# Query, key and relative rows of two attention layers: placed by DMA instead of by picks and moves

## The reference, cut to what matters

```python
q, k, v = heads(x @ wq + bq), heads(x @ wk + bk), heads(x @ wv + bv)     # 12 x 256 x 16 each
attn = einsum("bqd,bkd->bqk", q * scale, k)                               # 12 x 256 x 256
rel_h = einsum("bhwc,hkc->bhwk", q.reshape(12, 16, 16, 16), Rh)           # Rh[h, k] = rel_pos_h[h - k + 15]
rel_w = einsum("bhwc,wkc->bhwk", q.reshape(12, 16, 16, 16), Rw)
attn = attn.reshape(12, 16, 16, 16, 16) + rel_h[..., :, None] + rel_w[..., None, :]
out = softmax(attn.reshape(12, 256, 256)) @ v                             # back to 256 x 192, then @ wo + bo
...
x = x + L0(_gn(x)); x = x + L1(_gn(x))                                    # _gn: group norm, 32 groups
```

## Time and profile before

| | |
|---|---|
| median of 3 runs | 72.73 us (72.13 to 75.06) |
| the profiled execution's own time | 72.31 us |
| its span, first to last instruction | 70.6 us |
| mean granted TensorE clock | 0.992 |
| PE / ACT / DVE / GpSimd busy | 62.8 / 49.2 / 48.5 / 26.6 us |
| DMA | 1.75 MB in 1575 packets |

### The profile page before, as it was taken

One profiled execution on the slowest core, in us unless ns is written; L12 is line 12 of the kernel. 1 busy time (PEld: TensorE's weight loads), 2 busy tenths in 40 slices (PEclk: granted clock), 3 DMA queues, 4 the chain that ended last, 5 costly groups with the idle time before them and its releaser, 6 DMA issues.

```text
span 70.6 us, 1570 instructions
## 1 busy us (share of the span) xinstructions
PE 62.8 (89%) x574; PEld 51.5 (73%) x574; DVE 48.5 (69%) x110; ACT 49.2 (70%) x92; POOL 26.6 (38%) x61
## 2 busy tenths in 40 slices
PE   4996989999998999899997899999988998989950
PEld 4995869999767776655786769999766896555640
DVE  3789498999999993414258578999999886224420
ACT  2973194789999999992421096679999999993410
POOL 4846899998033135999405000000023132000000
PEclk9999999999999999999999999999999999999996
DMA  0789600000000000000000000000000000000003
GB/s 0 178 248 238 164 0 9 0 0 0 5 0 0 0 0 9 5 0 0 0 0 0 14 0 0 0 0 0 0 0 0 9 0 0 0 0 0 0 0 111
DMA packets 1575, 1.75 MB, mean 25 GB/s; under 512 B 344, under 2 KB 1178, under 8 KB 1568
## 3 DMA queue, kind: packets, MB, share of 16 engines
q1 hardware_dynamic: 1280, 1.49, 8.1%
q10 hardware_dynamic: 288, 0.16, 0.8%
HBM read 1.46 MB, written 0.20 MB: 23 GB/s over the span
## 4 chain that ended last, share of the span: by engine, by line
PE 56%; ACT 24%; DVE 12%; issue 4%
ACT pt L383 12%; PE ps L813 11%; ACT qs L336 10%; PE ps L681 5%; PE ps L728 5%; PE ps L596 4%; PE ps L794 4%; DVE zq L564 4%; PE ps L650 3%; PE ps L667 3%; PE ps L784 3%; PE ps L766 3%; PE ps L636 3%; PE ps L769 2%; PE ps L745 2%
## 5 line engine op out<-in xcount | busy, mean ns | idle before, releaser
L336 ACT ACTIVATE qs<-ps 64x512 fp32r<-64x512 f32 (+1 forms) x30 | 17.7, 590 | 0.8
L481 DVE TENSOR_REDUCE nm<-ps 128x2 f32<-128x512 f32 x24 | 15.5, 687 | 1.2 <-PE ps L681 0.8
L316 POOL CAST nmhl<-nm 128x4 fp32r<-128x4 f32 x12 | 2.3, 189 | 25.3 <-DVE nm L481 25.3
L681 PE MATMUL ps<-ks,qs 128*128 128x256 f32 x48 | 10.4, 305 | 0.9 <-DVE nm L481 0.3
L383 ACT ACTIVATE pt<-ps 128x1024 f32<-128x1024 f32 x10 | 10.3, 1027 | 0.2
L709 PE MATMUL ps<-qs,ks 128*128 128x256 f32 x48 | 9.4, 298 | 0.9 <-ACT qs L336 0.9
L681 PEld LDWEIGHTS ps<-ks,qs 128*128 128x128 f32 x48 | 7.1, 188 | 2.9 <-issue 2.6
L709 PEld LDWEIGHTS ps<-qs,ks 128*128 128x128 f32 x48 | 6.8, 189 | 1.7 <-issue 1.6
L794 PE MATMUL ps<-xn,win 97*128 97x256 f32 (+1 forms) x24 | 5.7, 385 | 1.3 <-DVE xn L542 1.3
L336 ACT ACTIVATE zq<-ps 64x256 fp32r<-64x256 f32 x6 | 2.3, 380 | 5.8 <-PE ps L794 5.7
L336 ACT ACTIVATE rr_hi<-ps 64x384 fp32r<-64x384 f32 x8 | 3.9, 485 | 3.3 <-PE ps L813 3.1
(11 more groups left out here) (105 smaller groups left out, 124.1 us busy)
## 6 DMA issues: line engine op xcount, KB each, us to landing
win<-in_w_in_dram SPq DMA_DIRECT2D x4, 216.0 KB
xt<-in_x_dram SPq DMA_DIRECT2D x2, 96.0 KB, 2.3
wout<-in_w_out_dram SPq DMA_DIRECT2D x2, 96.0 KB
wout<-in_w_out_dram SPq DMA_DIRECT2D x2, 48.0 KB
out_dram<-res ACTq DMA_DIRECT2D x1, 96.0 KB, 1.7
out_dram<-res SPq DMA_DIRECT2D x1, 96.0 KB, 1.7
rel_raw<-in_rel_dram ACTq DMA_DIRECT2D x1, 62.0 KB, 2.5
win<-in_w_in_dram SPq DMA_DIRECT2D x2, 2.2 KB
```

Source lines behind the costliest of these rows:

```text
L336: return act.activation(dst, src, ACT.Copy, scale=scale)
L481: dve.tensor_reduce(nm[:, p, a, :], ps[:, S_BANK[a], :].rearrange("p (t k) -> p t k", k=T), AX.X, ALU.max, negate=True).then_inc(max_sb, 1)
L681: last = mm(ps[:, S_BANK[a], t * T:(t + 1) * T], qs[:, 2 * p + a, t * P:(t + 1) * P], ks[:, 2 * p + a, :], start=True, stop=True)
```

## The change

- Picks and moves stay for the queries and keys of group 0 and for the relative terms of groups 0 and 1. The relative terms of group 0 now go to two banks and are moved in quarters (`("r", 0, odd, u)`, 64x256).
- The queries and keys of groups 1 and 2 are written by SP to DRAM tensors (`q_rows`, `k_rows`), twice each, since `qs` and `ks` hold every part twice, and read back into rows 0 to 63 of `qs` and `ks`.
- The relative terms of group 2 go from `rr_hi` and `rr_lo` straight to `qs`, by eight DMAs of 31 rows of 1 KB (SBUF to SBUF). GpSimd clears rows 64 and 65 of that group first (`clear_max_rows`).
- The output channels of the query and key weights are put in another order on the host (`by_channel`), so that a head's rows lie 4 apart.
- `values` goes from DVE to ACT; the maximum rows of pairs 3 and 5 go from ACT to DVE; a bias row of `ont` is set by GpSimd; the two normalising steps are split (`sums`, `normalise`).
- SP waits for the weights of layer 0 before it issues the loads behind them.
- The lists of PE, ACT and DVE get new orders.

```diff
+        K_BANK, Q_BANK, R0_BANK, R1_BANK = 1, 0, [2, 0], 1
-        ACT_MOVES = [("k", 0, 0), ("k", 1, 0), ("q", 1, 0), ("q", 1, 1), ("r", 0, 0), ("r", 1, 1),
-                     ("q", 2, 1), ("r", 1, 0), ("q", 2, 0), ("r", 2, 0), ("r", 2, 1), ("k", 2, 1)]
-        DVE_MOVES = [("q", 0, 0), ("q", 0, 1), ("k", 0, 1), ("k", 1, 1), ("r", 0, 1), ("k", 2, 0)]
+        ACT_MOVES = [("q", 0, 1), ("k", 0, 1), ("r", 0, 0, 0), ("r", 0, 1, 1), ("r", 1, 1), ("r", 1, 0)]
+        DVE_MOVES = [("q", 0, 0), ("k", 0, 0), ("r", 0, 1, 0), ("r", 0, 0, 1)]
+        MAX_ON_ACT, MAX_ON_DVE = [0, 1, 2, 4], [3, 5]
...
+        q_rows, k_rows = ([nc.dram_tensor(f"{name}_rows{l}", (64, G4, NG - 1, T), F32).ap() for l in range(LAYERS)]
+                          for name in "qk")
...
                 if l == 0:
+                    sp.wait_ge(ld_win[0], 48)
                     sp.dma_start(lora_ab[:, :, :], lora).then_inc(ld_lora, 16)
...
+            def queries_out(l):
+                sp.wait_ge(z_lo, 6 * l + NG)
+                for copy in range(2):
+                    sp.dma_start(q_rows[l][32 * copy:32 * copy + 32, :, :, :].rearrange("c j g t -> (c j) g t"),
+                                 zq[:, 1:NG, :].bitcast(F32)).then_inc(q_out, 16)
+
+            def keys_out(l, part):
+                sp.wait_ge((z_hi, z_lo)[part], 6 * l + 2 * NG)
+                for copy in range(2):
+                    first = 32 * part + 16 * copy
+                    sp.dma_start(k_rows[l][first:first + 16, :, :, :].rearrange("c j g t -> (c j) g t"),
+                                 zk[64 * part:64 * part + 64, 1:NG, :].bitcast(F32)).then_inc(k_out, 16)
+
+            def queries_in(l, g):
+                sp.wait_ge(q_out, 32 * (l + 1))
+                sp.dma_start(qs[0:64, G4 * g:G4 * g + G4, :].bitcast(F32),
+                             q_rows[l][:, :, g - 1, :]).then_inc(q_in[g - 1], 16)
+
+            def keys_in(l, g):
+                sp.wait_ge(k_out, 64 * (l + 1))
+                sp.dma_start(ks[0:64, G4 * g:G4 * g + G4, :].bitcast(F32),
+                             k_rows[l][:, :, g - 1, :]).then_inc(k_in[g - 1], 16)
+
+            def relative_in(l, part):
+                sp.wait_ge((rr_hi_sb, rr_lo_sb)[part], 4 * l + 4)
+                rr, first = ((rr_hi, 66), (rr_lo, 97))[part]
+                for j in range(G4):
+                    sp.dma_start(qs[first:first + R, 2 * G4 + j, :].bitcast(F32),
+                                 rr[G4 + j:P:G4, 2, :].bitcast(F32)).then_inc(r_in, 16)
+
+            for l in range(LAYERS):
+                queries_out(l)
+                keys_out(l, 0)
+                keys_out(l, 1)
+                for g in range(1, NG):
+                    queries_in(l, g)
+                    keys_in(l, g)
+                relative_in(l, 0)
+                relative_in(l, 1)
...
+            def clear_max_rows(l):
+                pool.wait_ge(rstd_sb, NC * (l + 1))
+                pool.memset(qs[64:66, 2 * G4:NH, :].bitcast(F32), 0.0).then_inc(max_zero, 1)
+                pool.wait_ge(max_zero, l + 1)
...
             def scores(l, p, a):
...
-                moved(l, *both("k", p // 2), *both("q", p // 2), *both("r", p // 2))
+                    moved(l, *both("k", 0), *both("q", 0))
+                if p < 2:
+                    moved(l, ("r", 0, 0, p), ("r", 0, 1, p))
+                elif p < 4:
+                    pe.wait_ge(q_in[0], 16 * (l + 1))
+                    pe.wait_ge(k_in[0], 16 * (l + 1))
+                    moved(l, *both("r", 1))
+                else:
+                    pe.wait_ge(q_in[1], 16 * (l + 1))
+                    pe.wait_ge(k_in[1], 16 * (l + 1))
+                    pe.wait_ge(r_in, 16 * 2 * G4 * (l + 1))
+                    pe.wait_ge(max_zero, l + 1)
```

More of the change, by code:

```diff
@@ L130, in attention_layers @@
         rstd_sb = sem("rstd_sb")
+        made_bias_row = sem("made_bias_row")
+        q_out, k_out, r_in, max_zero, nmt_dve, r0_ps = (sem(n) for n in (
+            "q_out", "k_out", "r_in", "max_zero", "nmt_dve", "r0_ps"))
+        q_in = [sem(f"q_in{g}") for g in range(1, NG)]
+        k_in = [sem(f"k_in{g}") for g in range(1, NG)]
         lora_zero, lora_sb = sem("lora_zero"), sem("lora_sb")
@@ L406, in _ @@
                 relative_rounded(l, 0)
+                move(l, 0)
                 relative_rounded(l, 1)
-                move(l, 0)
+                move(l, 1)
                 relative_rounded(l, 2)
-                move(l, 1)
                 relative_rounded(l, 3)
-                for n in range(2, 11):
-                    move(l, n)
+                move(l, 2)
+                move(l, 3)
+                move(l, 4)
+                values(l)
+                move(l, 5)
                 max_rows(l, 0)
-                move(l, 11)
                 max_rows(l, 1)
[L417 to L429, removed]
+                probabilities(l, 0)
+                max_rows(l, 2)
+                probabilities(l, 1)
+                probabilities(l, 2)
+                max_rows(l, 4)
+                probabilities(l, 3)
+                probabilities(l, 4)
+                last_probabilities(l, 0)
+                last_probabilities(l, 1)
+                last_columns(l)
+                turned(l, 0)
+                turned(l, 1)
             act.wait_ge(y_ps, NC + 1)
@@ L476, in normalise, with maximum, max_rows @@
                     rinv[:, g, :, :].unsqueeze(3).to_broadcast([P, TT, G4, D]), ALU.mult).then_inc(on_sb, 1)
[L478 to L482, removed]
+            def maximum(l, p, a):
+                dve.wait_ge(s_ps, NH * l + 2 * p + a + 1)
+                dve.tensor_reduce(nm[:, p, a, :], ps[:, S_BANK[a], :].rearrange("p (t k) -> p t k", k=T),
+                                  AX.X, ALU.max, negate=True).then_inc(max_sb, 1)
+            def max_rows(l, p):
+                dve.wait_ge(nmt_ps, PAIRS * l + p + 1)
+                dve.tensor_copy(*max_args(p)).then_inc(nmt_dve, 1)
             def relative_rest(l, n):
@@ L569, in _ @@
                 relative_rest(l, 1)
-                move(l, 2)
                 relative_rest(l, 2)
                 relative_rest(l, 3)
+                move(l, 2)
                 move(l, 3)
[L574 to L580, removed]
+                maximum(l, 0, 0)
+                maximum(l, 0, 1)
+                maximum(l, 1, 0)
+                maximum(l, 1, 1)
+                maximum(l, 2, 0)
+                maximum(l, 2, 1)
+                maximum(l, 3, 0)
+                maximum(l, 3, 1)
+                maximum(l, 4, 0)
+                maximum(l, 4, 1)
+                max_rows(l, 3)
+                maximum(l, 5, 0)
+                maximum(l, 5, 1)
                 out_columns(l, 0)
+                max_rows(l, 5)
+                out_columns(l, 1)
+                sums(l, 0)
+                sums(l, 1)
                 normalise(l, 0)
-                out_columns(l, 1)
                 normalise(l, 1)
+                sums(l, 2)
                 normalise(l, 2)
@@ L664, in relative_rows, with first_relative_rows @@
                 pick, rr, split = ((pick_rh, rr_hi, rr_hi_sb), (pick_rl, rr_lo, rr_lo_sb))[part]
                 pe.wait_ge(split, 4 * l + 4)
+                return mm(where, pick[:, 2 * u:2 * u + 2, :].rearrange("p j n -> p (j n)"), rr[:, g, :],
+                          stop=(part == 1), skip_group_check=True, **flags)
+            def first_relative_rows(l, part, u):
+                if part == 0 and u == 0:
+                    pe.wait_ge(pick_zero, 3)
+                    pe.wait_ge(z_lo, 6 * l + 6)
+                elif part == 0:
+                    moved(l, *both("q", 0))
+                last = relative_product(l, 0, part, u, ps[:, R0_BANK[u], 0:T], start=(part == 0))
+                if part == 1:
+                    last.then_inc(r0_ps, 1)
@@ L666, in relative_rows @@
+            def relative_rows(l, part):
+                if part == 0:
+                    moved(l, *both("k", 0))
                 for u in range(2):
-                    last = mm(ps[:, R_BANK[g], u * T:(u + 1) * T],
-                              pick[:, 2 * u:2 * u + 2, :].rearrange("p j n -> p (j n)"), rr[:, g, :],
-                              start=(part == 0 and u == 0), stop=(part == 1), skip_group_check=True)
+                    last = relative_product(l, 1, part, u, ps[:, R1_BANK, u * T:(u + 1) * T],
+                                            start=(part == 0 and u == 0))
```

171 lines of the change are left out of this document (84 added, 87 removed).

## The result

The kernel with the change takes 95.8 us, median of 4 runs (95.0 to 96.08), against 73.85 of the kernel before beside it (72.13 to 75.06). The ratio is 1.318, interval 1.313 to 1.324: slower by 32%. (The ratio leaves out the two slow executions of the kernel before, 74.97 and 75.06, since a program here has a second, slower state in some of its executions.) The profiled execution took 96.08 us, its span is 94.4; the span before was 70.6. So where 16 us more were forecast, 23 to 24 came. The sign, the place and the range held, the size did not.

What follows compares the result with a forecast made beforehand. Bound by when the first maximum starts, ACT's work and pair 4's first product, which eight one-engine DMAs would delay by 7.5 us: 72.3 + 2 x 7.5 + 2 x 0.5 = 88.3 us. Range 73 to 97, the forecast's own 79.7 to 96.7.

Steps and rivals of the forecast that it cites:

- Each of these DMAs runs on one engine, and all eight on the same: Group 2's relative rows: 31 is a prime, so 248 packets of 49 ns on one engine take 12.2 us.
- the spread: Rival for the eight 31-row DMAs: spread over 16 engines, two rows each, landing at 21.2; 66.9 us in all; chance 0.18.
- the serial case: Rival: the one-engine DMAs don't overlap and each pays 1.4 us of its own, 11 more per layer, 110 us; chance 0.02.
- The cheap packets: Rival: one engine, but SBUF to SBUF costs half, some 25 ns a packet, full at 24.4, 73.3 us; chance 0.06.
- The bounds of 38 and 60 ns: Price of a 1 KB packet on one engine, around the 49 taken: 248 packets from 9.4 to 14.9 us.
- They start behind group 2's reads, at 18.9: Start of the 31-row DMAs' data in SP's list, or an us earlier if writes run faster; `r_in` full at 31.4.
- the 12.2 of the sum: Time of the eight 31-row DMAs: 248 packets of 49 ns on one engine, 12.2 us.
- The 14.9: DRAM round trip: writes of queries and keys, issued from 10.3, data from 11.3, landed at about 14.9.
- between nothing and 2 us per layer: Behind the stall, products start at the 0.50 clock (1.2 GHz) after PE idles ten us; 0.5 us per layer taken.
- Hidden, by 1.3 us: Pair 2: group 1's reads landed at 17.7, wanted at 19.0, so the DRAM round trip costs nothing.
- so it costs nothing: SP's new wait for layer 0's weights puts the loads' issues off by some 3 us, to about 10.2, without cost.
- The first part: Less work on PE, ACT and DVE: 2.7 us gained per layer if every DMA came in time, lost in the stall.

Runs made afterwards that it cites:

- E2: Changed kernel with four DMAs of 64 or 60 source rows, onto 16 or 15 rows of four heads, for the eight of 31: 75.09 us, ratio 1.037.
- E3: Changed kernel with the first four 31-row DMAs left whole and the last four each cut into 16 and 15 rows: 87.53 us.
- E1: Changed kernel with each of the eight 31-row DMAs cut into one of 16 and one of 15 rows: 90.33 us.
- E6: Changed kernel with the last four 31-row DMAs issued by ACT on its own queue instead of SP: 95.67 us.
- E7: Changed kernel with group 2's relative rows back on PE picks and ACT moves, queries and keys still by DMA: median 72.26 us against 72.53.
- E5: Changed kernel with 180 unused filler products on PE in the stall ahead of pair 4's first product: 92.24 us.
- E8: E7 with SP's new wait for the weights taken out and eight filler products ahead of pair 2: 70.78 us against 72.5, ratio 0.976.
- E10: E2's four DMAs with E8's two edits (no new wait for the weights, eight fillers): median 74.09 us against 72.16.
- E9: E8 with the queries written to DRAM once and read into both halves by two DMAs: 70.69 us, ratio 0.975.

## Why the prediction was right or wrong

**The order of the argument held.** The views pointed to the start of the first maximum, ACT's share and pair 4's first product, and it is at this product that the time was lost. "Each of these DMAs runs on one engine, and all eight on the same" is shown by three things that don't hang on each other: the packet count (5184, and 5292, 5424 and 5664 in E2, E3 and E1, each exact), the plateau of 22 GB/s at a share of 0.07, and E6, in which it stays though the DMAs come from two queues and are all issued. E2 shows the size: 20.7 us go with the 31. Of the rivals, the spread (66.9) and the serial case (110) fall with the count and the plateau. The cheap packets (25 ns) fall with 1024 B / 22.5 GB/s = 45 ns; I took 49. The bounds of 38 and 60 ns were those of 768-byte packets, not brought to 1 KB; nothing came of it.

**The step that failed: "They start behind group 2's reads, at 18.9".** They ran from 21.8. One engine's 248 x 45 = 11.2 us, 1.0 less than the 12.2 of the sum, end at 33.0, and pair 4 runs at 33.69, not 31.4: 2.9 later at the start, 1.0 shorter, and 0.7 in place of 0.3 from the last row to the product. The 2.9 has two parts. First, the writes were put as landed at 14.9, but SP passed its wait for the keys at 16.3. The 14.9 is the end of the data (11.3 + 3.6); of the fixed 2.0 us only 1.0 had been used ahead of them, and the landing was left out. Second, the three reads behind that wait, 256 KB each, would be 2.4 us at the loads' 334 GB/s, and the sum gave them 2.0 (16.9 to 18.9); they took 3.8, from 18.0 to 21.8, at 195 GB/s in 19 to 21. The loads fill tiles of 96 and 128 rows, the reads 64 partitions; that the partitions, or the rows gathered from DRAM with a stride, are the reason was not tried and is open. The 31-row DMAs beside them are not the reason: E7 has none, and its reads ran at 204 and 187 GB/s in 19 to 20 and 20 to 21.

**The mis-sized term: the clock.** It was put "between nothing and 2 us per layer", with 0.5 taken. E5 measures 1.7, and the tail grew by 2.1 in layer 0. Its argument was that ACT and DVE lead the first 4 us; the windows show PE busy for 3.00 of 3.00 us at 36 to 39 with the clock at 0.59. At 1.2 GHz, as I read it, PE becomes the engine that leads. The upper bound would have been the better value: four `turn_max` products took 0.63 there, and 0.40 at the full clock.

The sum by these values: 72.3 + 2 x (33.69 - 23.89) + 2 x 2.08 = 96.1, against the profiled execution's 96.08. It uses layer 0 for both; in layer 1 the two parts differ by some tenths. These are values of the same trace, so the sum shows only that the two parts are the whole. Of the 7.8 us that 88.3 was short, the late start and end of the rows are 4.6 (2 x 2.3) and the tail 3.2 (2 x 1.6).

**"Hidden, by 1.3 us" was wrong in layer 0, without a cost here.** The maximum that pair 2 wants (the third, not the fourth as written) was done at 18.9, as forecast; PE had `turn_max` until 19.63, and pair 2 began at 20.14. The ten us of stall swallowed that half us. In the profiled execution of E7, without the stall, the same lateness shows as 0.85 us of idle PE. It comes from the writes and reads above, and perhaps from the new wait for the weights, "so it costs nothing": it puts six loads between 7.7 and 10.2, right ahead of the 1 MB of writes. The four key issues take 3.36 us in layer 0 and 2.42 in layer 1, where no loads are near. But the traces don't settle it: SP passed its wait for the keys at 15.79 to 16.57 in the eight kernels with the wait for the weights, and at 15.56, 15.73 and 16.23 in the three without it (E8, E10, E9).

**The first part was right in direction.** The first product is at 16.42 (16.6 was forecast) and the first maximum at 16.93 (17.0). The gain of 2.7 us per layer "if every DMA came in time" was had by no run: the best version traced at the full clock, E8, gets 1.35 at pair 4 and 1.0 at the layer's end, with the relative moves back on ACT. It had been said that the gain is lost in the stall; so it was.

## What to carry to other kernels

Count the completion packets of a DMA before you cost it: 31 rows, which have no divisor up to 16 but 1, put the whole transfer on one engine, at 22 GB/s, and cutting them costs SP 0.7 to 0.8 us for each further issue, so reshape the transfer (64 rows onto 16 rows of four heads) rather than split it. Behind a stall of several us, cost the first us of the next stage at half the TensorE clock (five us of it here, 1.7 us lost). Rows placed by DMA must be wanted late; those wanted soonest, last in a long list of DMAs, belong on the engines: with the relative rows back on PE, the loads ahead of the writes and eight fillers, the same change gives 2.4%.

## What the runs showed of the hardware that was not expected

- SP's issue of a DMA from SBUF to SBUF takes 0.64 us (2.56 / 4) for 31 rows and 0.74 (5.96 / 8) for 16 or 15, against 0.41 for a write of 256 KB (0.82 / 2). With DMAs waiting on the one engine, it rises to 1.42 (5.70 / 4), which I read as SP being held back by them; how many must wait was not tried. E6 has 3.70 / 4 = 0.93 on SP while ACT issues beside it.
- DMA reads of 1 KB rows into 64 partitions ran at 195 GB/s with a share of 1.13, and, 256 KB each, landed 4.2 and 4.7 us after their issue where the 98 KB load took 2.3.
- Filler products of the same shape took 0.057 us each in E5 (10.22 / 180), but 0.113 at the start of the kernel before (28 in 3.17 us), where the windows show the clock at 1.00 too. So here the granted clock of the first microseconds does not tell the rate at which the products run.
- One kernel's granted clock differs between executions: E7 had one at 1.00 (70.6 us) and three at 0.97 to 0.98 (72.1 to 72.8), E8 five at 1.00 and one at 0.95 (73.5), the kernel before mostly 0.99 to 1.00 (72.0 to 72.7) and once in a while 0.954 (75.4). What decides it was not found.
